# Quantised 3x3 convolutions from one fp32 image instead of three bf16 parts, side taps as row-tile pairs

## The reference

```python
# layer 0: spatial attention over N = 1024 positions, then two 1x1 convolutions summed
scores = einsum('bci,bcj->bij', c_, b_);  A = softmax(scores, axis=1)
e = x + alpha * einsum('bcj,bkj->bck', d_, A);  x = conv1x1(e, wd1, bd1) + conv1x1(e, wd2, bd2)
# layer 1: two 3x3 convolutions, weights rounded to integers of 3 bits (times alpha),
# each followed by batch normalisation with statistics of the batch
h = relu(bn(conv3x3(x, lsq(w1)))); x = relu(bn(conv3x3(h, lsq(w2))) + x)
# layer 2: two 3x3 convolutions, weights on 16 levels, taps (0,0) and (2,2) masked to zero
h = act_quant(bn_eval(conv3x3(x, wq1)))          # round(clip(., 0, 1) * 15) / 15
x = act_quant(bn_eval(conv3x3(h, wq2)) + x)
# layer 3: 1x1 bottleneck to 16 channels, bn, relu, 64 box filters, bn, relu(x + .)
```

## Time and profile before

| | us |
|---|---|
| timed runs | 250.59, 257.62, 360.6 |
| median | 257.62 |
| span of the profiled execution | 254.0 |
| busy PE, DVE, ACT, POOL | 193.2, 198.4, 113.2, 101.1 |
| mean granted TensorE clock | 0.898 of full speed |

### The profile page before, as it was taken

How to read it: one execution, slowest core, us unless ns; L and a number is a source line. 1 busy time by engine, 2 the same in 40 slices (tenths; PEclk the granted TensorE clock), 3 DMA queues, 4 the chain that set the end, 5 groups by cost and what they waited for, 6 DMA issues and landing times.

```text
span 254.0 us, 3239 instructions
## 1 busy us (share of the span) xinstructions
PE 193.2 (76%) x1176; PEld 76.0 (30%) x1193; DVE 198.4 (78%) x382; ACT 113.2 (45%) x170; POOL 101.1 (40%) x63
## 2 busy tenths in 40 slices
PE   5885998979986898780599697374796969998930
PEld 1352343323321232220122132111332313457820
DVE  3198669999999469999989665789997899853374
ACT  2354782729435483520374220069300897215315
POOL 4064868647434333499401510494310482000000
PEclk9799999999999599996599889657998897999995
DMA  7970000000000000000000000000000000000004
GB/s 157 250 228 0 0 3 0 1 0 1 3 0 0 0 0 3 1 0 1 0 0 3 0 0 0 0 0 0 3 0 1 0 0 3 1 3 3 3 1 165
DMA packets 1952, 5.29 MB, mean 21 GB/s; under 512 B 272, under 2 KB 656, under 8 KB 1808
## 3 DMA queue, kind: packets, MB, share of 16 engines
q1 hardware_dynamic: 1504, 4.66, 6.5%
q10 hardware_dynamic: 432, 0.43, 0.8%
HBM read 4.04 MB, written 1.05 MB: 20 GB/s over the span
## 4 chain that ended last, share of the span: by engine, by line
DVE 46%; PE 29%; issue 16%; ACT 4%; DMA 2%; DVEq 0%; SPq 0%; POOL 0%; ACTq 0%; POOLq 0%
DVE parts L890 8%; DVE nmax L998 6%; PE ps L390 5%; PE ps L409 5%; DVE dz L882 5%; DVE res L899 3%; PE ps L443 3%; DMA xd<-x 2%; DVE parts L904 2%; DVE st L1077 2%; PE ps L323 2%; DVE wtmp L939 2%; PE ps L564 2%; ACT parts L606 2%; PE ps L363 2%
## 5 line engine op out<-in xcount | busy, mean ns | idle before, releaser
L606 ACT ACTIVATE probs<-ps,nmax 128x1024 f32<-128x1024 f32 x32 | 35.6, 1114 | 59.2 <-DVE nmax L998 59.1
L409 PE MATMUL ps<-probs,dz 128*64 128x512 f32 x128 | 36.5, 650 | 22.9 <-DVE dz L882 22.9
L998 DVE TENSOR_REDUCE nmax<-ps 128x1 f32<-128x1024 f32 x32 | 38.9, 1217 | 11.5 <-PE ps L390 9.9
L390 PE MATMUL ps<-c,b 128*128 128x512 bf16 x167 | 42.7, 390 | 0.6 <-issue 0.3
L443 PE MATMUL ps<-parts,wq 128*128 128x512 bf16 x115 | 34.0, 422 | 7.4 <-DVE parts L904 5.9
L890 DVE COPY parts<-parts 64x480 bf16<-64x480 bf16 x50 | 33.4, 669 | 4.6 <-ACT parts L606 3.1
L1261 POOL TENSOR_TENSOR parts<-res,parts 128x512 bf16<-128x512 f32 x12 | 14.4, 1196 | 55.2 <-DVE parts L904 55.2
L390 PEld LDWEIGHTS ps<-c,b 128*128 128x128 bf16 x174 | 15.6, 100 | 34.4 <-issue 16.0
L882 DVE TENSOR_SCALAR dz<-d,rz 128x64 f32<-128x64 f32 x32 | 20.1, 627 | 1.1
L443 PEld LDWEIGHTS ps<-parts,wq 128*128 128x128 bf16 x120 | 10.7, 103 | 28.9 <-issue 11.8
L409 PEld LDWEIGHTS ps<-probs,dz 128*64 128x64 f32 x128 | 6.6, 139 | 37.9 <-DVE dz L882 32.3
(11 more groups left out here) (208 smaller groups left out, 335.0 us busy)
## 6 DMA issues: line engine op xcount, KB each, us to landing
xd<-x SPq DMA_DIRECT2D x8, 256.0 KB, 8.0
wraw<-wconv SPq DMA_DIRECT2D x1, 1152.0 KB, 11.7
out<-box_t SPq DMA_DIRECT2D x4, 256.0 KB, 2.3
consts<-cst SPq DMA_DIRECT2D x1, 322.0 KB, 6.5
parm<-par ACTq DMA_DIRECT2D x1, 163.0 KB, 4.7
wsp<-wa ACTq DMA_DIRECT2D x1, 128.0 KB, 2.8
wsrc<-wa ACTq DMA_DIRECT2D x1, 128.0 KB, 6.0
```

The source lines that it names most:

```text
L390: last = mm(o[:, 512 * h:512 * h + 512], w[:, b % 2, j], m[:, b % 2, 512 * h:512 * h + 512], start=w is b11, stop=w is b31)
L409: last = mm(y[64 * p:64 * p + 64, :], dz[:, g % 4, :], probs[:, g % 3, 512 * p:512 * p + 512], start=False, stop=t == JT - 1)
L606: return nc.scalar.activation(o, i, f, **kw)
L998: V.tensor_reduce(nmax[:, i:i + 1], slot(("S", i)), AX.X, ALU.min).then_inc(max_ready, 1)
```

## The change

The parts, the shifted copies and their weights go. One fp32 image `img` is kept with a row pitch of 17 elements (16 and one zero), so that the neighbour column is a read at an offset of one element. Weights `wq` become fp32. Each main tap is one fp32 matmul 128 x 128 x 512 on rows of 16 elements. Each side tap reads only one half of the partitions, so two of different images and different PSUM banks are issued one behind the other on partitions 64 to 127 and 0 to 63 of the array (`side_taps(k, even, odd)`), and `swap_images` waits, before the roles of the two images change, until both banks were written. For the warm-up and `keep_busy` a bf16 array `spin` of 512 elements is read. ACT writes the image once, and the fp32 copy `y_of` as well for k = 0 and 2 only.

```diff
-        wq = sb("wq", [4, 6, 128], BF16)
-        parts = sb("parts", [3, NB, 2, PAD], BF16)
-        wside = sb("wside", [3, 3, 2, 64], BF16)
-        res = sb("res", [2, HALF])
+        wq = sb("wq", [4, 6, 128])
+        img = sb("img", [NB, PAD])
+        spin = sb("spin", [512], BF16)
...
+        def image(b, kh=1, ds=0, q=slice(0, 128)):
+
+            first = 1 + PITCH * kh + ds
+            return img[q, b, first:first + H * PITCH].rearrange("q (r s) -> q r s", s=PITCH)[:, :, 0:S2]
...
+            def convolve(k, b, begin=True):
+
+                arrived(k, b)
                 for kh in range(3):
-                    mm(bank, wq[:, k, kh, :], parts[:, i, b, 0, S2 * kh:S2 * kh + HALF],
-                       start=i == 0 and kh == 0, stop=False)
...
+                    mm(ps[:, BANKS[k % 2][b], :], wq[:, k, kh, :], image(b, kh),
+                       start=begin and kh == 0, stop=False)
+
+            def side_taps(k, even, odd, begin=False, stop=False):
+
+                n, down = (3, 0) if k < 2 else (2, 1)
+                for a in range(n):
+                    end = stop and a == n - 1
+                    o = mm(ps[:, BANKS[k % 2][odd], :], wq[64:128, k, 3 + a, :],
+                           image(odd, a + down, -1, slice(64, 128)), start=begin and a == 0, stop=end)
+                    e = mm(ps[:, BANKS[k % 2][even], :], wq[0:64, k, 3 + a, :],
+                           image(even, a, 1, slice(0, 64)), start=False, stop=end)
+                done = conv_done[k] if stop else sides_done
+                o.then_inc(done, 1)
+                e.then_inc(done, 1)
...
+            def convolve_rest(k):
+                side_taps(k, 0, 1)
+                convolve(k, 2)
+                swap_images()
+                side_taps(k, 1, 0, stop=True)
+                arrived(k, 3)
+                side_taps(k, 2, 3, begin=True)
+                convolve(k, 3, begin=False)
+                swap_images()
+                side_taps(k, 3, 2, stop=True)
...
-            convolve(0, 0, 0)
-            convolve(0, 0, 1)
             values(NB * JT - 2)
-            convolve(0, 0, 2)
+            convolve(0, 0)
             values(NB * JT - 1)
...
             bottleneck(0)
-            convolve(3, 2, 0)
+            convolve(3, 2)
             residuals(0, 0)
-            convolve(3, 3, 0)
+            convolve(3, 3)
+            side_taps(3, 2, 3)
             residuals(0, 1)
             bottleneck(1)
+            swap_images()
+            side_taps(3, 3, 2, stop=True)
             bottleneck(2)
...
-                run(main(0, b), src, func, **kw).then_inc(main_done[0], 1)
-                run(y_of[k][:, b, :], src, func, **kw).then_inc(gen[k], 1)
+                run(image(b), as_rows(src), func, **kw).then_inc(in_place, 1)
+                if k != 1:
+                    run(y_of[k][:, b, :], src, func, **kw).then_inc(gen[k], 1)
...
-            for b in range(NB):
-                side_copies(1, b, 0)
-                split_residual(1, b)
-                split_second(1, b)
-                if b:
-                    side_copies(1, b - 1, 2)
-            side_copies(1, NB - 1, 2)
             tanh_weights(3)
...
-                V.tensor_scalar(main(0, b), v, LEVELS, None, ALU.min).then_inc(q_ready, 1)
-                for half in range(2):
-                    o, moved = side(2, b, half, True)
-                    V.tensor_scalar(o, moved(v), LEVELS, None, ALU.min).then_inc(q_ready, 1)
+                V.tensor_scalar(image(b), as_rows(q_in[:, b % 2, :]), LEVELS, None, ALU.min).then_inc(q_ready, 1)
...
-            third_part(0, 1)
             edge(0, P_XMAX, K_IR1)
```

More of the change, by code:

```diff
@@ L222, in slot, with as_rows @@
             return ps[:, 2 * n:2 * n + 2, :].rearrange("q a n -> q (a n)")
[L224 to L242, removed]
+        y_of = (y1, None, y3)
+        def image(b, kh=1, ds=0, q=slice(0, 128)):
+            first = 1 + PITCH * kh + ds
+            return img[q, b, first:first + H * PITCH].rearrange("q (r s) -> q r s", s=PITCH)[:, :, 0:S2]
+        def as_rows(t):
+            return t.rearrange("q (r s) -> q r s", s=S2)
         x_in = sems("x_in", NB)
@@ L282, in build @@
         stored, f_out_dve = sem("stored"), sem("f_out_dve")
-        warm = main(0, 0)
+        warm = spin[:]
         block = ctx.enter_context(nc.Block())
@@ L459, in convolve @@
-                if i == last_part:
-                    last.then_inc(conv_done[k], 1)
+                    mm(ps[:, BANKS[k % 2][b], :], wq[:, k, kh, :], image(b, kh),
[11 more added lines that the diff above has]
+                e.then_inc(done, 1)
@@ L723, in outer_out @@
                 image_out(2, b, tmp[:, b % 2, :], ACT.Relu, bias=bn_b[:, 1:2])
-                act.wait_ge(main_done[0], 2 * NB + b + 1)
-                for half in range(2):
-                    o, moved = side(0, b, half, True)
-                    run(o, moved(main(0, b)), ACT.Copy).then_inc(side_done[0], 1)
-            def third_sides(b):
-                act.wait_ge(main_done[2], 2 * NB + b + 1)
-                for half in range(2):
-                    o, moved = side(2, b, half, True)
-                    run(o, moved(main(2, b)), ACT.Copy).then_inc(side_done[2], 1)
             def scaled(b):
@@ L912, in place_b @@
                     yield wq[q, k, 3:3 + nbw, o], src[q, NA:NA + 64 * nbw].rearrange("q (a n) -> q a n", n=64)
-            def side_weights(k):
-                dve.wait_ge(wq_ready[k], 5)
-                for half in range(2):
-                    q, o = slice(64 * half, 64 * half + 64), slice(64 * (1 - half), 64 * (1 - half) + 64)
-                    for to in (q, o):
-                        V.tensor_copy(wside[to, k, :, half, :], wq[q, k, 3:6, o]).then_inc(wq_ready[k], 1)
             def lsq_scales():
@@ L1112, in round_inner @@
                 dve.wait_ge(q_int, b + 1)
-                v = q_in[:, b % 2, :]
-                V.tensor_scalar(main(0, b), v, LEVELS, None, ALU.min).then_inc(q_ready, 1)
-                for half in range(2):
-                    o, moved = side(2, b, half, True)
-                    V.tensor_scalar(o, moved(v), LEVELS, None, ALU.min).then_inc(q_ready, 1)
+                V.tensor_scalar(image(b), as_rows(q_in[:, b % 2, :]), LEVELS, None, ALU.min).then_inc(q_ready, 1)
             def outer(b):
@@ L1330, in _ @@
             pool.wait_ge(hblk_zero, 1)
-            for k in (1, 2):
-                for b in range(NB):
-                    third_part(k, b)
 def constants():
```

144 lines of the change are left out of this document (35 added, 109 removed).

## The result

The changed kernel takes 259.58 us (median; 259.55, 259.55, 259.61, 262.82) where the kernel before takes 255.62 (median; 250.59, 253.62, 257.62, 360.6). The ratio of the fast runs, which leaves out those over 1.5% above the fastest of their kernel (257.62 and 360.6), is 1.032, 95% interval 1.021 to 1.044; the two medians as they stand would give 1.016. It is slower: its four times lie above every time of the kernel before but the 360.6, those beside the later experiments included (250.0 to 258.0). The profiled execution has a span of 257.7 and its own time is 259.55, so 1.8 us lie outside the span.

The account below looks back on a forecast made before the run. DVE was taken to set the pace in the attention and convolution 1, with little room for PE or DVE in convolutions 2 and 3. 254.0 - 15.8 + 3.8 - 1.1 + 20.7 = 261.6, so 262 us; range 250 to 283.

Parts of the forecast that it names:

- A pair at 0.9: Convolutions: two side-tap halves on different rows run beside each other, 0.9 us a pair; 1.8 if one after the other.
- Rival C: Convolutions: fp32 reads slower at a pitch of 17; 281 us if a quarter more, 272 if only pairs lose; chance 0.18.
- Attention -15.8: Attention from 66 us on: PE's waits for DVE's `dz` and slow clock shrink, 15.8 us less in four terms.
- (a): Attention, PE's wait at 71.09: two DVE copies ahead of `nmax` go, 1.3 us back.
- (b): Attention, wait at 83.68: splitting and `wside` copies go, and the slow clock with them; 3.2 + 2.9 = 6.1 us back.
- (c): Attention: POOL's `edge` additions stay but begin three tiles earlier, PE waiting 8.0 us in all; 5.3 us back.
- (d): End of the attention: 3.2 us of splitting and copies between the last tiles go; 3.1 us come back.
- Rival A: Attention, tiles 22 to 26: `edge` additions slip into DVE's gaps, 24.6 us saved instead of 15.8; 251 us; chance 0.27.
- Convolution 0, +5.0: Last attention product to first average: 18.0 us becomes 23.0 with fp32 main matmuls and pairs, 5.0 more.
- Normalisation 0, -1.2: First normalisation, 4.45 us: POOL is about five microseconds early, `bn_a`'s wait shrinks from 2.3 to about 1; 1.2 less.
- Convolution 1, -1.1: Convolution 1 to the second average: 27.5 us becomes 26.4, with 1.0 put in for a slow clock; 1.1 less.
- Convolutions 2 and 3, +20.7: First residual to `h_raw`: 29.7 us becomes 50.4 by fp32 work on PE and waits for ACT and DVE; 20.7 more.

Follow-up runs that it names:

- e8_same_rows: The changed kernel with both side-tap halves on partitions 0 to 63, the odd images' taps then computed from the wrong half; span 287.0 us.
- e3_bf16_all: The changed kernel with images and weights of all four convolutions in bf16, one matmul where there is one now; 205.41 us.
- e2a_dve_spare: The changed kernel plus spare DVE copies, subtractions and casts in the attention where the kernel before had such work, onto tiles nobody reads; span 267.5 us.
- e2b_dve_pool_spare: The changed kernel plus spare DVE work in the attention and POOL's spare third parts of three images, where the kernel before had them; span 276.5 us.
- e4_edges: The changed kernel with POOL's four edge additions apart: one ahead of all POOL work, two behind image 2's third part C, one behind image 3's; 257.3 us.
- e10_warm: 12 useless matmuls instead of 4 ahead of the first average, against the changed kernel with edge additions apart, convolution 3 in bf16 and three orders changed; 243.04 us.
- e6_orders: The changed kernel with three orders changed, on ACT, DVE and PE, in convolutions 2 and 3; 255.03 us, ratio 1.012 to the kernel before.
- e1_unpaired: The changed kernel with each call's side taps reordered: first all halves on partitions 64 to 127, then all on 0 to 63; span 260.9 us.

## Why the prediction was right

The forecast was 262 us and slower; 259.58 and slower is what came, by the mechanism it gave: 16 us out of the attention and a few out of the normalisation and convolution 1 do not pay for 4 + 20 us of fp32 work on PE.

- **A pair at 0.9**, halves in rows running beside each other: right (0.86, as a main matmul), and e8_same_rows shows that this carries 30 us of the forecast. The rule of four row tiles giving 3.07, which would have made the pairs 10.8 us dearer ("TensorE: Matmul & The Clock Gate", section "Measured speedup vs the span model", in the Trainium skill), doesn't show for two halves: 0.86 a pair, 0.86 for one half in e8_same_rows.
- **Rival C**, slower reads at a pitch of 17: wrong for fp32. The records of L420 start 0.43 apart, as those of the contiguous fp32 matmuls of the earlier trace rows do. (In e3_bf16_all, in bf16, those of L420 start 0.23 to 0.24 apart and contiguous ones 0.22; whether the pitch does that was not tried.) The five lines instead of four that were estimated from the Trainium skill ("SBUF — State Buffer", "Door 1: The DMA port swizzle") are not to be seen in PE's time here.
- **Attention -15.8**: -15.9 measured, and putting the work back gives it all back. But the sum is nearer than its terms. By the end of the same `dz` in both traces, cut at tiles 12, 14, 20 and 25, (a) was 1.7 and not 1.3, (b) 5.4 and not 6.1, (c) 6.4 and not 5.3, (d) 2.6 and not 3.1, and 0.2 was lost ahead of them: that the sum hit within 0.1 is luck. In (b) the cost of the `wside` copies was read as their own. e2a_dve_spare has them back and PE waits 0.53 there; the 3.18 came of their meeting POOL's `rb`, as the 3.42 in e2b_dve_pool_spare. In (c) the four waits at the `edge` additions were 5.9 and not 8.0. Behind the 3.72 the clock fell, from 110.6 to 114.0 us, about 1.7 lost, which the sum had not named; the kernel before lost about as much behind its 9.01 (clock 0.53 from 123.4 to 127.2). Rival A, additions that fall into gaps, is wrong: each of the four cost PE something, and so did the one that stands alone in e4_edges (0.51).
- **Convolution 0, +5.0**: +4.3. The 0.9 a matmul or pair was a little high (0.86; 0.8 for the 21 of them), the 0.15 a change a little low (0.2).
- **Normalisation 0, -1.2**: the step that failed most. It took POOL to be about five microseconds early at its second operation and left 1 us of wait behind it. In fact POOL's second operation ended at 143.1 and the `hblk` filling behind it at 145.0, six microseconds before the average, and the whole 2.5 went. e2b_dve_pool_spare makes POOL late again, and the stretch ahead of the average grows by 1.5. That DVE's `bn_a` waits for POOL was right as a mechanism; where POOL stands relative to DVE was misjudged.
- **Convolution 1, -1.1**: -1.9, again by the 0.9 that was too high; the slow clock that was put at 1.0 came, and cost 0.9 (27.5 against 26.6 in runs without it), by the `keep_busy` matmuls ahead of the first image (e10_warm).
- **Convolutions 2 and 3, +20.7**: +19.8. The 1.6 forecast for ACT's image came as 1.47. The 2.5 ahead of image 2 of convolution 3 (31.8 to 34.3) came as a wait of 1.72 for `xi` and a bottleneck of 0.7. PE's own work was shorter, by the same 0.9, and the end behind its last side taps 4.4 and not 3.9. e6_orders shows that the two waits are of order and not of the arithmetic.
- **Span and time**: the prediction left open how the span of before stood to its median and added nothing. The profiled run of after lies 1.85 above its span, and the single runs of the experiments 1.7 to 2.1. With that the sum would have read 263.4; the 3.9 by which the stages came out shorter were partly covered by it.

## What to carry to other kernels

Moving work from one engine to another is counted stage by stage: DVE's copying and splitting was worth 10 us in the stage where DVE set the pace and, by DVE's idle time there, nothing where PE became the longer, while PE's new work was paid in full wherever PE was the longer. Keep the dear type for the operand that needs it: integers stayed exact in bf16, and fp32 for them was 12.7 of the 20 us lost in the last two convolutions. Two half-height matmuls on different rows cost as one, and they need not be neighbours in the program; what costs is a run of more than two on the same rows before the others come. And where POOL holds DVE, a few tenths of a microsecond decide what it costs: behind the same four copies PE waited 0.53 or 3.42.

## What the runs showed that was not expected

PE's order is not strict between row halves. The even halves were held back by one matmul's time for a run of three (0.97) and by four for a run of six (3.55), in fp32; what stands behind two odd halves in the program starts beside the first.

POOL's additions of 3.64 us cost PE anything from 0.47 to 3.72, mostly by how long they hold the DVE operation that PE needs next; even an operation on two elements was held for 1.45 (e2b_dve_pool_spare).

The start moves. From one kernel to another the first product with `dz` came between 24.9 and 30.8 us after the first instruction, though the instructions up to there are nearly the same. The first eight fp32 matmul records on `xd` show the larger part, in the changed kernel, with convolution 3 in bf16 and with the edge additions apart:

```profile
6.93 3.70 PE L300 MATMUL ps<-xd,whalf 128*128 128x512 f32 x8 [1.64 <-DMA xd<-x]
```

```profile
7.40 6.62 PE L305 MATMUL ps<-xd,whalf 128*128 128x512 f32 x8 [1.77 <-DMA xd<-x]
```

```profile
8.06 5.14 PE L300 MATMUL ps<-xd,whalf 128*128 128x512 f32 x8 [3.08 <-DMA xd<-x]
```

In the second they start 0.85 apart, twice the usual 0.43, and 2.9 us are lost here, of a first product that is 3.1 later. That is the pace of the lower clock level; the granted clock of these microseconds is on record for the third alone, 0.83 from 6 to 16 us. There the input came 1.1 later, 1.4 went in these records and 1.3 in the wait for `bhalf`, 3.9 of 4.1 in all. Late inputs alone don't do it: in e1_unpaired the same records start at 7.81, 0.9 later than in the changed kernel, and its first product is earlier by 0.8.

These starts are 5.9 us apart, and the timed runs of before spread over 8.0 (250.0 to 258.0); whether the starts make that spread was not tried. Between the last product and the end the same stretch repeats within 0.1 us as long as the clock is full (22.27 to 22.29 from the last product to the first average, in seven kernels), which is why a stage can be read from one profile and a total can't.
